# A selective scan on one core: projections in two steps, B and C rows replicated by DMA, remainders from TensorE, two increments of twelve on GpSimd, y summed over four units in PSUM

## The reference

```
xs     = x as rows, x as columns, and both reversed            # 4 sequences of L = 1024
x_dbl  = xs @ x_proj_weight[k].T                               # 6 + 16 + 16 rows: z, B, C
dt     = softplus(dt_projs_weight[k] @ x_dbl[0:6] + bias)
h[n]   = h[n] * exp(dt * A[d, n]) + (dt * xs) * B[n]           # 16 states, one step per pixel
y      = sum over n of h[n] * C[n];   y += Ds * xs
```

## Time and profile before

| | us |
|---|---|
| median of three runs (3161.8 to 3197.0) | 3168.3 |
| the profiled execution: its time | 3164.3 |
| its span, first to last instruction | 3162.5 |
| busy over the span: PE / DVE / ACT / POOL | 2584.5 / 2241.6 / 1442.1 / 1309.5 |
| POOL product with C (L528), x384, one | 2.354 |
| DVE product with B (L558), x768, one | 0.673 |
| DVE scans (L614), x384 and x384, one | 1.210 and 1.269 |

### The profile page before, as it was taken

How to read it: one execution, slowest core, us unless ns; L and a number is a source line. 1 busy time by engine, 2 the same in 40 slices (tenths; PEclk the granted TensorE clock), 3 DMA queues, 4 the chain that set the end, 5 groups by cost and what they waited for, 6 DMA issues and landing times. The chain is left out here.

```text
span 3162.5 us, 37235 instructions
## 1 busy us (share of the span) xinstructions
PE 2584.5 (82%) x10794; PEld 961.9 (30%) x10794; DVE 2241.6 (71%) x3025; ACT 1442.1 (46%) x1949; POOL 1309.5 (41%) x676
## 2 busy tenths in 40 slices
PE   4777667666667777767666899999999889999999
PEld 2111111111111111111133233333333246666666
DVE  4999899999999989999754887776777541111112
ACT  3444444445444444445455166675767532222221
POOL 1788778788778877878732000000000110000000
PEclk9676777777767777776778699999999889999999
DMA  3455555555555555555414312211312300000000
GB/s 87 144 163 167 143 155 167 163 156 163 157 156 161 165 157 149 167 165 157 132 42 106 41 23 37 28 22 23 42 22 36 74 18 6 5 5 5 5 5 10
DMA packets 101529, 286.89 MB, mean 91 GB/s; under 512 B 14638, under 2 KB 18897, under 8 KB 101329
## 3 DMA queue, kind: packets, MB, share of 16 engines
q1 hardware_dynamic: 100266, 284.85, 34.1%
q10 hardware_dynamic: 1102, 0.19, 0.0%
HBM read 239.66 MB, written 25.88 MB: 84 GB/s over the span
## 5 line engine op out<-in xcount | busy, mean ns | idle before, releaser
L528 POOL TENSOR_TENSOR hs<-hs,bc 128x1024 f32<-128x1024 f32 x384 | 900.1, 2354 | 225.2 <-DVE hs L614 224.7
L501 ACT ACTIVATE decay<-decay,a_neg 128x1024 f32<-128x1024 f32 x384 | 440.6, 1148 | 647.5 <-DMA decay<-dt_rows 637.7
L425 PE MATMUL psU<-stack,spread_sel 96*128 96x512 bf16 x768 | 361.6, 487 | 418.1 <-DVE hs L614 347.4
L1426 DVE TENSOR_REDUCE mx<-ps 128x1 f32<-128x512 f32 x864 | 557.9, 685 | 159.9 <-PE ps L1259 143.7
L1401 ACT ACTIVATE P<-ps 128x512 f32<-128x512 f32 x768 | 431.4, 597 | 305.2 <-PE ps L1271 270.7
L558 DVE TENSOR_TENSOR psU<-psU,bc 128x512 f32<-128x512 f32 x768 | 514.7, 673 | 25.8 <-issue 13.6
L614 DVE TENSOR_TENSOR_SCAN hs<-decay,psU 128x512 f32<-128x512 f32 x384 | 464.6, 1210 | 69.5 <-PE psY L387 56.7
L614 DVE TENSOR_TENSOR_SCAN hs<-decay,hs,psU 128x512 f32<-128x512 f32 x384 | 487.4, 1269 | 1.1
L387 PE MATMUL psY<-hs,state_sel 128*32 128x512 f32 x1572 | 398.2, 848 | 23.8 <-DVE Y L571 11.5
L1699 DVE SCALAR_TENSOR_TENSOR acc<-psE,gate,acc 128x192 f32<-128x192 f32 x128 | 53.4, 417 | 448.5 <-PE psE L1599 445.6
L425 PEld LDWEIGHTS psU<-stack,spread_sel 96*128 96x128 bf16 x768 | 71.2, 100 | 984.4 <-DVE hs L614 809.1
(11 more groups left out here) (235 smaller groups left out, 2353.1 us busy)
## 6 DMA issues: line engine op xcount, KB each, us to landing
decay<-dt_rows SPq DMA_DIRECT2D x388, 512.0 KB
stack<-parts SPq DMA_DIRECT2D x297, 64.0 KB, 5.4
dt_rows<-dt SPq DMA_DIRECT2D x33, 384.0 KB, 7.2
qs<-qk_parts SPq DMA_DIRECT2D x90, 128.0 KB, 6.6
ks<-qk_parts SPq DMA_DIRECT2D x90, 128.0 KB, 7.1
qk_parts<-qparts SPq DMA_DIRECT2D x16, 576.0 KB, 3.7
w<-in_L_ffn_w_dram SPq DMA_DIRECT2D x8, 576.0 KB, 9.7
X<-in_x_dram SPq DMA_DIRECT2D x4, 768.0 KB, 11.2
```

The lines of the kernel that those rows point to most:

```text
L425: pe.matmul(psU[:, q % UR, :], s.spread_sel[:, gg, :], stack[:, ui % 2, j, CH * pos:CH * pos + CH], start=True, stop=True).then_inc(dtu_sp ...
L501: nc.scalar.activation(decay[:, t % DR, :], decay[:, t % DR, :], ACT.Exp, scale=s.a_neg[:, col:col + 1]).then_inc(decay_ready, 1)
L528: pool.tensor_tensor(h, h, bc[:, 2 * p + r, 1, :], ALU.mult).then_inc(hc_ready, 1)
L1426: v.reduce_max(mx[:, slot, u:u + 1], ps1[:, (slot * MAXES + u) % R, :], AX.X).then_inc(max_done, 1)
```

## The change

- `prepare`: instead of replicated `w_b`, `w_c` and a premultiplied `w_dt`, one weight `w_xd` gives all 38 rows of both senses at once (z of r = 0 at partition 0, of r = 1 at 32, B and C at 64 and 96), and `w_dt` is the second step, with 6 rows. New are a diagonal matrix with D (`d_diag`) and -1 times the identity in bf16 (`minus_bf`).
- `order`: f is now the slowest, then p, then r, so that four units in a row add to the same half.
- Projections: `inputs` makes `xd` for one orientation of an image (4 matmuls, at tile 1 of units 4 and 6), `steps` makes z from 6 of its rows. `xt` is gone; PE and POOL read X, and PE reads `hs`, through a turned view (`turned`).
- B and C: SP stores 64 rows of `xd` to DRAM and loads them back replicated (`load_bc`, two loads of 512 KB in units 5, 6, 7 and 0).
- Remainders: PE computes dtu - hi and dtu - hi - mid in `psP`; ACT casts them in halves. POOL's two subtractions go.
- Tiles 5 and 11 (`POOL_TILES`): dtu is stored as rows, loaded replicated (`load_rep`, 512 KB, one buffer `rep`), POOL multiplies it with B, ACT writes the tile's decay into `psU`, and DVE scans straight from there; no spread and no product.
- y: D*x and the sums of four units accumulate in `psY`, columns through a turned read of `hs`; ACT copies y out twice an image (`take`).
- `HR` 8 instead of 6; the waits for `summed` stand at tiles 2, 5, 8, 11. The DRAM tensor `dt_rows` has four slots instead of two.

The diff, cut to its core:

```diff
-        HR, DR, UR = 6, 4, 4
-        xt = sb("xt", [HC, 2, L])
+        HR, DR, UR = 8, 4, 4
+        POOL_TILES = (5, 11)
...
-            p, f, r = ui // 4, ui // 2 % 2, ui % 2
-            return p, f, r, p + 2 * r
+            f, p, r = ui // 4, ui // 2 % 2, ui % 2
+            return f, p, r, p + 2 * r
...
+                def inputs(out, nb, p, c):
+                    for h in range(2):
+                        m = pe.matmul(out, s.w_xd[:, p, h, :], turned(s.X[:, nb, h, :], p)[:, 16 * c:16 * c + 16, :],
+                                      start=(h == 0), stop=(h == 1))
+                    m.then_inc(xd_proj, 1)
+                def steps(nu, c):
+                    f, p, r, k = order(nu)
+                    pe.matmul(psP[0:HC, c, :], s.w_dt[BLK * r:BLK * r + R, p, HC * f:HC * f + HC],
+                              xd[BLK * r:BLK * r + R, p, CH * c:CH * c + CH], start=True, stop=True).then_inc(z_proj, 1)
+                def remainder(c, known, ready):
+                    cs = slice(CH * c, CH * c + CH)
+                    m = pe.matmul(psP[0:HC, c, :], s.ident[0:HC, 0:HC], dtu[:, cs], start=True, stop=False)
+                    for i in range(known):
+                        m = pe.matmul(psP[0:HC, c, :], s.minus_bf[:], parts[:, i, cs], start=False, stop=(i == known - 1))
+                    m.then_inc(ready, 1)
+                def skip(b, f, c):
+                    pe.matmul(psY[0:HC, c, :], s.d_diag[:, f, :], s.X[:, b, f, CH * c:CH * c + CH], start=True, stop=False)
+                def sum_states(n, ui, trip, c):
+                    p = order(ui)[1]
                     if c == 0:
-                        if trip == 0 and r == 0:
-                            pe.wait_ge(y_taken, pair + (1 + START))
                         pe.wait_ge(hc_ready, n * TILES + (TILES + 3 * trip + 3 + START))
                     for j in range(NBLK):
+                        h = hs[:, (ui * TILES + 3 * trip + j) % HR, :]
+                        h = h.rearrange("p (w h) -> p h w", h=HH) if p else h.rearrange("p (h w) -> p h w", h=HH)
                         m = pe.matmul(psY[BLK * j:BLK * j + BLK, c, :], s.state_sel[:, trip, :],
-                                      hs[:, (3 * trip + j) % HR, CH * c:CH * c + CH],
-                                      start=(trip == (first or 0) and (r == 0 or first is not None)),
-                                      stop=(trip == SUB - 1 and r == 1))
...
+                                if t not in POOL_TILES:
+                                    pe.wait_ge(scan_done, g + (S0 - UR + 1))
+                                    pe.matmul(psU[:, q % UR, :], s.spread_sel[:, gg, :],
+                                              stack[:, ui % 2, j, CH * pos:CH * pos + CH],
+                                              start=True, stop=True).then_inc(dtu_spread, 1)
...
+                                if t == 5:
+                                    if c == 0:
+                                        pe.wait_ge(z_taken, n * 2 + 4)
+                                        if ui in XD_UNITS:
+                                            pe.wait_ge(xd_ready, b * 4 + (2 * XD_UNITS[ui] + 6))
+                                        pe.wait_ge(dtu_ready, n + 2)
+                                        pe.wait_ge(hi_ready, n + 2)
+                                    remainder(c, 1, rest_ready)
+                                if t == 7:
+                                    pe.wait_ge(mid_ready, n * 2 + (c + 3))
+                                    remainder(c, 2, tail_ready)
+                                if t == 9:
+                                    if c == 0:
+                                        pe.wait_ge(xd_ready, nb * 4 + (2 * order(nu)[1] + 2))
+                                    pe.wait_ge(lo_ready, n * 2 + (c + 3))
+                                    steps(nu, c)
...
+                def part(i, n1, c, rest, ready):
+                    act.wait_ge(rest, n1 * 2 + (c + 1))
+                    nc.scalar.copy(parts[:, i, CH * c:CH * c + CH], psP[0:HC, c, :]).then_inc(ready, 1)
...
+                            to = at = decay[:, t % DR, :]
+                            if t in POOL_TILES:
+                                to = psU[:, 2 * t % UR:2 * t % UR + 2, :]
+                                if r:
+                                    to = to[:, ::-1, :]
+                                at = at.rearrange("p (c l) -> p c l", c=2)
+                                act.wait_ge(scan_done, n * (2 * TILES) + (2 * t - 2 + S0))
                             act.wait_ge(landed[t % DR], n * (16 * TILES // DR) + (16 * (t // DR) + 16))
-                            nc.scalar.activation(decay[:, t % DR, :], decay[:, t % DR, :], ACT.Exp,
+                            nc.scalar.activation(to, at, ACT.Exp,
                                                  scale=s.a_neg[:, col:col + 1]).then_inc(decay_ready, 1)
-                            bc_side(t, b, ui, n)
-                            split_side(t, n + 1, b, ui)
-                            z_side(t, unit_ahead(b, ui)[1], n + 2)
...
+                            if t + 3 in POOL_TILES:
+                                i = POOL_TILES.index(t + 3)
+                                pool.wait_ge(rep_landed, n * (16 * len(POOL_TILES)) + (16 * i + 16))
+                                pool.tensor_tensor(rep[:], rep[:], bc[:, slot, 0, :], ALU.mult).then_inc(rep_ready, 1)
...
                                 pool.tensor_tensor(dt[:], dt[:], soft[:], ALU.add).then_inc(dt_ready, 1)
                             if t == 11:
+                                pool.wait_ge(tail_ready, n * 2 + 4)
+                                pool.wait_ge(dtu_stored, n * 32 + 64)
                                 pool.wait_ge(dt_ready, n + 3)
-                                if np_:
-                                    pool.wait_ge(xt_half, nb * 2 + 2)
                                 pool.sem_inc(dtu_begun, 1)
-                                pool.tensor_tensor(dtu[:], dt[:], source(nb, np_)(nf, 0, L),
-                                                   ALU.mult).then_inc(dtu_ready, 1)
+                                pool.tensor_tensor(dtu[:].rearrange("p (a e) -> p a e", a=HH),
+                                                   dt[:].rearrange("p (a e) -> p a e", a=HH),
+                                                   turned(s.X[:, nb, nf, :], np_), ALU.mult).then_inc(dtu_ready, 1)
...
-                            v.wait_ge(dbu_ready, g + 1)
+                            if t in POOL_TILES:
+                                da, du = psU[:, q % UR, :], rep[:, cs]
+                                if q % 2 == 0:
+                                    v.wait_ge(rep_ready, n * len(POOL_TILES) + (POOL_TILES.index(t) + 1))
+                            else:
...
+                def keep_dt(slot):
+                    sp.dma_start(s.dt_dram[slot], dt[:]).then_inc(dt_stored, 16)
+                def keep_dtu(slot):
+                    first = rows_of(POOL_TILES[0])
+                    step = rows_of(POOL_TILES[1]) - first
+                    src = dtu[first:first + DD, :]
+                    sp.dma_start(s.dtu_dram[slot, 0], src).then_inc(dtu_stored, 16)
+                    sp.dma_start(s.dtu_dram[slot, 1], dtu[first + step:first + step + DD, :]).then_inc(dtu_stored, 16)
+                def keep_xd(p):
+                    sp.dma_start(s.bc_dram[p], xd[64:128, p, :]).then_inc(xd_stored, 16)
+                def load_dt(slot, t):
+                    d = rows_of(t)
+                    src = s.dt_dram[slot, d:d + DD, :].unsqueeze(1).broadcast_to([DD, N, L])
+                    sp.dma_start(decay[:, t % DR, :], src).then_inc(landed[t % DR], 16)
+                def load_rep(slot, i):
+                    src = s.dtu_dram[slot, i].unsqueeze(1).broadcast_to([DD, N, L])
+                    sp.dma_start(rep[:], src).then_inc(rep_landed, 16)
+                def load_bc(slot):
+                    p, r = slot // 2, slot % 2
+                    for i in range(2):
+                        at = BLK * r + N * i
+                        src = s.bc_dram[p, at:at + N, :].unsqueeze(0).broadcast_to([DD, N, L])
+                        sp.dma_start(bc[:, slot, i, :], src).then_inc(bc_landed[slot], 16)
...
                             sp.wait_ge(scan_done, n * (2 * TILES) + (2 * t + 2 + S0))
                             if t + DR < TILES:
-                                load(ui % 2, t + DR)
+                                load_dt(ui % 4, t + DR)
                             else:
-                                load((ui + 1) % 2, t + DR - TILES)
-                            if t in (4, 5, 7):
-                                part = (4, 5, 7).index(t)
-                                sp.wait_ge((hi_ready, mid_ready, lo_ready)[part], n + 2)
-                                stack_up(part, (ui + 1) % 2)
+                                load_dt((ui + 1) % 4, t + DR - TILES)
```

(66 more changed lines are left out.)

332 lines of the change are left out of this document (136 added, 196 removed).

## The result

The changed kernel takes **3281.9 us** (median of 4 runs, 3267.6 to 3298.4), the kernel before, on the same chip, 3176.5 us (4 runs, 3161.8 to 3197.0). The ratio is 1.0329, 95% interval 1.0248 to 1.041: slower, by 105 us where 259 were forecast. The two profiled executions lie 121 us apart (3285.3 and 3164.3 us). A ratio leaves out executions over 1.5% above the fastest of their kernel, while a median counts all.

A forecast was written before the change was run, and what follows sets the result against it. DVE and eight DMA engines were taken as both full. 15 loads at 3.35 us plus 3.2, 0.2 and 0.3 made 54.0 us a unit against 45.9, +259 us over 32 units on 3164: about 3420 us, range 3290 to 3560.

The forecast's parts named there:

- The side: Whole kernel: it would get slower, by 259 us.
- DVE's work: Scan loop: two tiles without products save 2.0 us a unit, Y additions moved to PSUM and ACT 0.8.
- The wait for the sums: DVE waiting for PE's sums, 1.8 us a unit, goes because eight state buffers replace six.
- The floor of 41.0 us: DVE's time a unit after the change, 45.6 - 2.0 - 0.8 - 1.8; were DVE the bound, -157 us.
- Turned reads: PE's state sums: ACT's factor 1.91 gives 16 units +11 us, 43.5, covered by 54; as a rival, chance 0.03.
- new loads join the same eight engines: Increment and B/C loads were priced like decay loads, whose eight-row sources keep them on eight of sixteen DMA engines.
- the price of a load: Loop DMA: a 512 KB load costs 3.35 us, between 2.56 and 4.03, so 15 loads set the unit's time.
- rival 1: Eight DMA engines run at 2.56 us a load: -93 us, 3070 us; chance 0.21 together with rival 4 and between.
- the loads of the pairs as one load a unit: Four slots of two B or C loads in eight units, counted as one 512 KB load a unit, 15 in all.
- costed PE as "even": PE's matmuls lost and gained in a unit balance, leaving 32.4 us busy.
- The prologue: Before the loop, B and C go over DRAM and eight projections go: 0, between -5 and +8 us.
- What was to show it: Profile after: share 0.55 to 0.58, unit near 54 us, decay waits 10 us a unit, DVE busy under 80%.

The follow-up runs named there:

- experiment 4: Changed kernel, rows stored twice, loads of 16 rows by 8 copies: 3211.1 us; B/C pair also split: 3117.6; PE's step also at tile 10: 3084.5.
- Experiment 1: Kernel before plus three unused 512 KB loads a unit: 3224.7 us (ratio 1.017); plus five such loads: 3333.6 us (1.055).
- experiment 3: Changed kernel, second B/C load of each pair behind tile 8: 3200.9 us; PE's next-unit step also moved from tile 9 to 10: median 3171.9 us.
- experiment 6: Changed kernel, split-part loads issued ahead of three first decay loads and the rep load: 3276.1 us; same edit on the 3084.5 us kernel: 3095.0 us.

## Why the prediction was right and wrong

**Right.** The side, and that it is the decays on which DVE would wait where the kernel before hardly did. DVE's work: 2.7 us a unit less, 2.8 forecast. The wait for the sums is gone. The floor of 41.0 us without late loads: units of 40.2 to 42.3 us (experiment 4). Turned reads are covered; their factor is 1.17 (1151/981), where 1.91 was taken. That new loads join the same eight engines: the share stayed at 0.55. The Trainium skill, DMA: Bandwidth & Descriptors, section "Rules for kernel authors", says that a leading zero-stride broadcast of c copies confines a DMA to at most c engines. The traces agree: the share is 0.56 in the 20 us behind a pair, and 0.85 in the loop once the sources of the decay and increment loads have 16 rows.

**The step that failed** is the price of a load: "Today's mean: 45.9 x 0.97 = 44.5 us of work ... I take 3.35". It reads the share as use. But the loop before was bound by DVE, so its mean rate of 158 GB/s is the demand and says nothing of what eight engines can do; the share was full all the same, with transfers that took longer (217 ns for 4 KB, 193 after). The changed kernel's own unit of 49.1 us leaves 3.05 us a load with all its waits counted in. Experiment 1 gives at most 2.7 to 2.8 us in the place of 3.35, and 15 x 2.7 + 3.4 = 43.9 us of DMA work, or 45.4 with 2.8. That is under the 45.9 from which rival 1 would decide, but close to it, and above DVE's 41.0. So on eight engines the change is about even, as the median of experiment 3 has it. The forecast put that rival's point at 2.83 us and gave it too little, with the row at 205 GB/s in hand.

**Why it was slower all the same.** Not by mean capacity, but by order, where it meets slow stretches of the eight engines: the pair of B and C loads in front of the decays (some 70 us, shown by experiment 3), and PE's step behind ACT's low part at tile 9 (shown by moving it: 35 us more by the medians and 62 by the ratios, 1.0115 to 0.9919, on eight engines; 33 us on sixteen). How much of the 70 us comes from the place in the queue, and how much from fewer slow stretches once the pair is apart, is not shown. The prediction counted the loads of the pairs as one load a unit, spread evenly where two come at once in four units of eight, and costed PE as "even" by its busy time, without asking what its order waits for. In both cases something is queued behind a late arrival, and the prediction did not follow that queue. With both mended the loss is gone (median 3171.9 us, the five shortest executions 3144.8), but rival 1's 3070 us is not reached: in the execution that was traced, DVE still waits 144.4 us for decays.

**The prologue**, costed at 0 (-5 to +8), was too low as well: the start is 14.6 us late, of which little reaches the end (experiment 6).

**What was to show it**: a unit near 54 us (49.1), waits for decay of 10 us a unit (4.0), DVE busy under 80% (81.4%): none came. Share 0.55 and ACT waiting for DMA came, and would have come with rival 1 too: they were no test. That the side was right is in part luck: the decays came late, but not because the queue was over its mean capacity, as the sum had it.

## What to carry to other kernels

The mean rate of a transfer queue in a loop that another engine bounds is the loop's demand, not the queue's capacity, whatever its busy share says; add spare loads until the time moves, and read the capacity there. Average load is half of the question: ask of each added transfer and each moved instruction what stands right behind it, since two large loads in a row cost some 70 us more here than the same loads six tiles apart. Before a change is given up, try its parts in another order: here two orders took the +3.3% away, and with a wider source the time is 2.5% under the kernel before (1.7% under it with the same source). Look at more than one execution before calling the rest a gain.

## What the runs showed of the hardware

The same eight DMA engines, at nearly the same share of 0.51 to 0.56, moved between 130 GB/s (before, 12 us) and 205 GB/s (before, 2 us; 202 over 20 us after). The mean time of one 4 KB transfer, counted over the traces from 95 to 1500 us, is about 217 ns before, 193 after and 175 with five spare loads. That mean is a mixture. Cut into pieces of 2 us, the loop before has a mean under 175 ns in 16% of them and of 250 ns or more in 35%; after it is 41% and 17%, with the pair apart 51% and 9%, with five spare loads 67% and 5%. So more loads came with fewer slow stretches. The time of a transfer hardly follows how much is queued (correlation of 0.08 to 0.23 over these pieces, in those traces and that with three spare loads). What sets it stays open. Eight engines reached 201 GB/s over a loop with five spare loads; sixteen reached 245 in a stretch of 12 us, less than the double, and their ceiling was not sought.
